# An AdaLN, RWKV and mixture-of-experts block: routing weights spread over 64 partitions by DMA in place of selection products

## The reference, cut to what matters

```
logits = x @ gate_w.T                                  # (n, 8)
topk_vals, topk_idx = jax.lax.top_k(logits, 2)
w = jax.nn.softmax(topk_vals, axis=-1)
comb = jnp.zeros((n, E), x.dtype).at[jnp.arange(n)[:, None], topk_idx].add(w)
g = jnp.einsum('nh,ehm->enm', x, Wg)                   # 8 experts of M = 64
u = jnp.einsum('nh,ehm->enm', x, Wu)
eo = jnp.einsum('enm,emh->enh', jax.nn.silu(g) * u, Wd)
y = jnp.einsum('ne,enh->nh', comb, eo)
y = y + jax.nn.silu(x @ sWg) * (x @ sWu) @ sWd         # the shared expert, 128 wide
```

## Time and profile before

| what | value |
|---|---|
| runs shown | 423.52, 424.86, 425.09 us; median 424.86 us |
| profiled execution, its own time | 426.54 us |
| its span in the profile | 424.7 us |
| mean granted TensorE clock | 0.954 of full speed |
| TensorE busy | 377.9 us, 89% of the span |
| VectorE busy | 334.4 us, 79% |
| ScalarE busy | 294.6 us, 69% |
| GpSimd busy | 53.0 us, 12% |
| DMA moved | 13.27 MB, mean 31 GB/s |

### The profile page before, as it was taken

The page is one execution under the profiler, slowest core; times in us unless marked ns, Lnnn a source line. Parts: engine busy times, 40 slices in busy tenths (PEclk is TensorE's granted clock), DMA queues, the critical chain, the costliest instruction groups (busy, mean ns, idle before and its releaser), DMA issues.

```text
span 424.7 us, 4271 instructions
## 1 busy us (share of the span) xinstructions
PE 377.9 (89%) x1347; PEld 223.3 (53%) x1347; DVE 334.4 (79%) x661; ACT 294.6 (69%) x466; POOL 53.0 (12%) x80
## 2 busy tenths in 40 slices
PE   0796196399999999999999999999999999979985
PEld 0745142375546564646465645565465546645742
DVE  1597979896989799869988898969897988661541
ACT  1576949974899479956996699848993787334332
POOL 2111344000220013000500050002200200010000
PEclk9996579689999999999999999999999999989999
DMA  7900001000100020001100110002000100100011
GB/s 269 264 1 2 1 0 49 0 2 0 50 0 2 0 99 2 2 0 55 45 0 2 51 49 0 2 14 85 2 1 0 49 2 0 49 2 0 0 51 49
DMA packets 15626, 13.27 MB, mean 31 GB/s; under 512 B 4690, under 2 KB 15092, under 8 KB 15604
## 3 DMA queue, kind: packets, MB, share of 16 engines
q1 hardware_dynamic: 14464, 11.94, 9.2%
q10 hardware_dynamic: 1140, 1.06, 0.8%
HBM read 8.80 MB, written 4.19 MB: 31 GB/s over the span
## 4 chain that ended last, share of the span: by engine, by line
PE 73%; ACT 14%; DVE 7%; issue 3%; DMA 1%; ACTq 1%; POOL 0%; DVEq 0%
PE mm L707 19%; PE mm L602 18%; PE yo L735 17%; PE yo L620 7%; PE yo L629 3%; ACT mixed L381 3%; PE cb L719 2%; PE tp L556 2%; ACT yT L448 2%; ACT L480 2%; ACT sgm L428 1%; DMA rows<-in_L_attn_bo_dram 1%; ACT arg L387 1%; PE yo L783 1%; ACT pool_g L434 1%
## 5 line engine op out<-in xcount | busy, mean ns | idle before, releaser
L602 PE MATMUL mm<-mixed,WT 128*128 128x512 f32 x192 | 89.0, 603 | 3.8 <-DVE mixed L845 3.8
L735 PE MATMUL yo<-act,w_dn 128*128 128x512 f32 x160 | 73.0, 605 | 3.8 <-DVE act L1022 3.8
L707 PE MATMUL mm<-h_h,w_up_h 128*128 128x512 f32 x160 | 61.0, 463 | 1.4 <-DVE h_l L945 1.4
L602 PEld LDWEIGHTS mm<-mixed,WT 128*128 128x128 f32 x192 | 34.7, 189 | 45.2 <-issue 40.0
L735 PEld LDWEIGHTS yo<-act,w_dn 128*128 128x128 f32 x160 | 30.3, 194 | 39.7 <-issue 35.0
L707 PE MATMUL mm<-h_l,w_up_h 128*128 128x512 f32 x160 | 51.2, 401 | 0.0
L707 PE MATMUL mm<-h_h,w_up_l 128*128 128x512 f32 x160 | 51.0, 400 | 0.0
L370 ACT ACTIVATE kv<-mm,cols 128x512 f32<-128x512 f32 x32 | 22.0, 688 | 39.6 <-PE mm L602 39.6
L290 POOL TENSOR_TENSOR n_ve<-n_mv,small 128x4 f32<-128x4 f32 x16 | 6.8, 424 | 304.8 <-DVE n_mv L834 304.8
L620 PE MATMUL yo<-pool_n,WT 128*128 128x512 f32 x64 | 31.9, 646 | 8.2 <-DVE pool_n L923 5.7
L845 DVE SCALAR_TENSOR_TENSOR mixed<-hT,cols,mixed 128x512 f32<-128x512 f32 x48 | 37.3, 821 | 0.5 <-ACT mixed L381 0.5
(11 more groups left out here) (143 smaller groups left out, 672.6 us busy)
## 6 DMA issues: line engine op xcount, KB each, us to landing
x_in<-in_L_attn_x_dram SPq DMA_DIRECT2D x8, 512.0 KB, 3.5
out_dram<-pool_x SPq DMA_DIRECT2D x5, 512.0 KB, 2.9
pool_x<-in_L_wmod_dram SPq DMA_DIRECT2D x2, 512.0 KB, 6.4
out_dram<-x_third SPq DMA_DIRECT2D x2, 512.0 KB, 2.9
pool_x<-in_L_wmod_dram SPq DMA_DIRECT2D x2, 256.0 KB, 4.4
pool_g<-in_L_ffn_Wg_dram SPq DMA_DIRECT2D x2, 256.0 KB, 7.6
pool_g<-in_L_ffn_Wu_dram SPq DMA_DIRECT2D x2, 256.0 KB, 5.6
w_dn<-in_L_ffn_Wd_dram SPq DMA_DIRECT2D x1, 512.0 KB, 4.2
```

The lines of the kernel that those rows point to most:

```text
L602: last = nc.tensor.matmul(mm[PROJECT_BANK[j]][:, :], WT[:, w, kc, oc * P:(oc + 1) * P], mixed[:, w, kc, :], start=(kc == 0), stop=(kc == K ...
L707: last = nc.tensor.matmul(mm[UP_BANK[i]][:, :], w[:, kc, gu, e * P:(e + 1) * P], rhs[:, kc, :], start=(n == 0), stop=(n == 3 * KH - 1))
L735: last = nc.tensor.matmul(yo[oc][:, :], w_dn[:, e, oc * P:(oc + 1) * P], act[:, e, :], start=(e == 0), stop=(e == NB - 1))
```

## The change

The two float32r halves, the matrix `sel` and the four products per chunk go. `comb` is kept as one float32 value (8 columns), `combT` has 8 partitions, and eight DMAs per chunk, issued by SyncE, copy each row of `combT` (one partition, 512 floats, 2 KB) to 64 partitions of a new SBUF tile `weights`. `weigh` reads `weights` and waits for the two DMAs of its block (`spread_in`). Two steps of `route` go, and `turn2` waits for `combT_done` where it waited for `act_done`, since `tp` and `cb` are no longer read by `weigh`. The new function `spread(n)` stands on SyncE ahead of `store(n - 1)` and `load(n + 3)`.

```diff
             def store(c):
                 sp.wait_ge(x2_done, 2 * (c.n + 1))
                 sp.dma_start(out_chunks[c.n], x1[c.n % 3][:, :, :]).then_inc(stored[c.n % 3], 16)
+
+            def spread(c):
+
+                sp.wait_ge(combT_done, c.n + 1)
+                for i in range(NP):
+                    wait(sp, act_done, NP * (c.n - 1) + i + 1)
+                    for e in range(2):
+                        sp.dma_start(weights[e * M:(e + 1) * M, i, :],
+                                     combT[2 * i + e:2 * i + e + 1, :].unsqueeze(1).to_broadcast([1, M, CH])
+                                     ).then_inc(spread_in[i], 16)
...
-            for n in range(NC - 1):
+            for n in range(NC):
+                spread(chunk(n))
+                if n:
+                    store(chunk(n - 1))
                 if chunk(n + 3):
                     load(chunk(n + 3))
-                store(chunk(n))
...
             def comb_out(c):
                 ac.wait_ge(comb_turned, c.n + 1)
-                nc.scalar.activation(combT[:, :], cb[0:2 * E, :], ACT.Identity).then_inc(combT_done, 1)
+                for i in range(NP):
+                    wait(ac, spread_in[i], 32 * c.n)
+                nc.scalar.activation(combT[:, :], cb[0:E, :], ACT.Identity).then_inc(combT_done, 1)
...
                 pe.wait_ge(norm2.xn_done, TT * (c.n + 1))
                 if c.n:
-                    pe.wait_ge(act_done, NP * c.n)
+                    pe.wait_ge(combT_done, c.n)
...
-            def spread_comb(c, e):
-
-                if e == 1:
-                    pe.wait_ge(combT_done, c.n + 1)
-                elif e < 4:
-                    pe.wait_ge(act_done, NP * c.n + e - 1)
-                nc.tensor.matmul(comb_bank[e][:, :], sel[:, e - 1, :], combT[:, :], start=True, stop=True
-                                 ).then_inc(comb_mm, 1)
...
-                    elif n == 16:
-                        ins = V.tensor_tensor(pr, w1m, w2m, ALU.add)
-                    elif n == 17:
-                        ins = V.tensor_copy(comb[:, :, 0:E], pr)
                     else:
-                        V.tensor_tensor(comb[:, :, E:2 * E], pr, comb[:, :, 0:E].bitcast(F32), ALU.subtract
-                                        ).then_inc(comb_done, 1)
+                        V.tensor_tensor(comb[:, :, :], w1m, w2m, ALU.add).then_inc(comb_done, 1)
                         return
...
             def weigh(c, e):
-                ve.wait_ge(comb_mm, NP * c.n + e)
+                ve.wait_ge(spread_in[e - 1], 32 * (c.n + 1))
                 ve.wait_ge(prod_done, NB * c.n + e + 1)
-                nc.vector.tensor_tensor(act[:, e, :], comb_bank[e][:, :], sg[:, e, :], ALU.mult).then_inc(act_done, 1)
+                nc.vector.tensor_tensor(act[:, e, :], weights[:, e - 1, :], sg[:, e, :], ALU.mult).then_inc(act_done, 1)
```

More of the change, by code:

```diff
@@ L59, in adaln_rwkv_moe @@
         ident = sb("ident", [P, P])
-        sel = sb("sel", [2 * E, NP, P], F32R)
         prio = sb("prio", [P, TT, E])
@@ L100, in adaln_rwkv_moe @@
         r1 = sb("r1", [P, 7, TT])
-        comb = sb("comb", [P, TT, 2 * E], F32R)
-        combT = sb("combT", [2 * E, CH], F32R)
+        comb = sb("comb", [P, TT, E])
+        combT = sb("combT", [E, CH])
+        weights = sb("weights", [P, NP, CH])
         lgT = sb("lgT", [2 * E, CH])
@@ L117, in adaln_rwkv_moe @@
         sg = pool_g[:, :].rearrange("p (e n) -> p e n", e=NB)
-        sel_f = tmp[0:2 * E, 0, :].rearrange("p (i n) -> p i n", i=NP)
         rec = arg[:, 0, :, :]
@@ L127, in adaln_rwkv_moe @@
         cb = ctx.enter_context(nc.psum_tensor("cb", [P, CH], F32))
-        comb_bank = {1: cb, 2: cb, 3: cb, 4: tp}
         UP_BANK = (0, 1, 2, 3, 0, 3, 0, 1, 2, 0)
@@ L157, in adaln_rwkv_moe @@
             sem(n) for n in ("rows_in", "mod_in", "mod2_in", "sq_in", "up_in", "dn_in", "gw_in"))
-        consts_done, ident_done, sel_done = sem("consts_done"), sem("ident_done"), sem("sel_done")
+        consts_done, ident_done = sem("consts_done"), sem("ident_done")
         cols_turned, cols_done, cond_done, fall_done, consts2_done = (
@@ L202, in adaln_rwkv_moe @@
         combT_done = sem("combT_done")
-        comb_mm = sem("comb_mm")
+        spread_in = [sem(f"spread_in{i}") for i in range(NP)]
         up_mm = sem("up_mm")
@@ L216, in adaln_rwkv_moe @@
         bias_cols = (col["bk"], col["bv"])
-        ROUTE_STEPS = 18
+        ROUTE_STEPS = 16
         N_CONSTS2 = 4
@@ L269, in _ @@
             nc.gpsimd.memset(ident[:, :], 0.0).then_inc(consts_done, 1)
-            nc.gpsimd.memset(sel_f[:, :, :], 0.0).then_inc(consts_done, 1)
             nc.gpsimd.memset(small[:, 0, :], EPS).then_inc(consts_done, 1)
@@ L273, in _ @@
             nc.gpsimd.memset(small[:, 2, :], 0.0).then_inc(consts_done, 1)
-            pool.wait_ge(consts_done, 5)
+            pool.wait_ge(consts_done, 4)
             nc.gpsimd.affine_select(out=ident[:, :], in_=ident[:, :], compare_op=ALU.not_equal, fill=1.0,
                                     base=0, pattern=[[-1, P]], channel_multiplier=1).then_inc(ident_done, 1)
[L278 to L284, removed]
             def rstd(norm, c):
@@ L667, in turn_comb @@
                 for t in range(TT):
-                    last = nc.tensor.transpose(cb[0:2 * E, t * P:(t + 1) * P], comb[:, t, :].bitcast(F32),
-                                               ident[:, :])
+                    last = nc.tensor.transpose(cb[0:E, t * P:(t + 1) * P], comb[:, t, :], ident[:, :])
                 last.then_inc(comb_turned, 1)
@@ L712, in spread_comb @@
             @of_chunk
-            def spread_comb(c, e):
-                if e == 1:
-                    pe.wait_ge(combT_done, c.n + 1)
-                elif e < 4:
-                    pe.wait_ge(act_done, NP * c.n + e - 1)
-                nc.tensor.matmul(comb_bank[e][:, :], sel[:, e - 1, :], combT[:, :], start=True, stop=True
-                                 ).then_inc(comb_mm, 1)
-            @of_chunk
             def down(c, oc):
@@ L763, in step @@
                 up(prev, 7)
-                spread_comb(prev, 1)
                 up(prev, 8)
                 turn_attn(cur)
-                spread_comb(prev, 2)
                 project(nxt, (2,))
                 up(prev, 9)
-                spread_comb(prev, 3)
                 project(nxt, (3,))
-                spread_comb(prev, 4)
                 project(nxt, (4, 5))
@@ L1068, in _ @@
             nc.vector.memset(hT[0][:, :, 0:1], 0.0)
-            ve.wait_ge(sel_done, 2)
-            nc.vector.tensor_copy(sel[:, :, :], sel_f[:, :, :])
             ve.wait_ge(cols_turned, 1)
```

## The result

The change makes the kernel slower: 686.63 us (four runs, 683.27 to 687.83) against 424.84 us, a ratio of 1.616 with a 95% interval of 1.6094 to 1.6225. 701 us were forecast, in a range of 620 to 820.

What follows compares the result with a forecast made beforehand. TensorE was taken as the bound (89% busy, 44.7 us steps). Waiting for eight transfers per chunk at 5.0 us each adds 276.5 us to 426.54, giving 703.0, less 1.7 for the median: 701 us, range 620 to 820.

Steps and rivals of the forecast that it cites:

- s: Price of one 131,072-byte weights transfer from one SBUF partition, taken as 5.0 us; the forecast covers 3.8 to 6.8 us.
- The estimate of 685 us: Alternative whole time from the skill's 27.6 GB/s for partitions 0 to 3: 4.75 us per transfer, about 685 us.
- W: End of `weigh` 4 on VectorE: T + 11.95 before, forecast T + 47.5 with store and load, T + 42.0 without load.
- behind the last two Ws: After chunk 7's last `weigh`, the cold clock of the last products was to add 1.7 us.
- T: End of ScalarE's write of `combT` in a step, 195.38 us in the pattern step; offsets count from it.
- the cold clock: TensorE's products after some 10 us idle run at the lower of two clocks, costing 1.9 us at `down`.
- Issued at once: All eight transfers of a chunk issued together, about 0.4 us per issue; block i's weights land at T + 1.4 + 10 i.
- Rival 1: Sixteen engines read one partition side by side, 1.15 us gained per step in six full ones: 419 us, chance 0.09.
- VectorE has slack for `weigh` 1: Rival 1's step on VectorE: `weigh` 1 waits 0.6 us, W slips to 207.9, `down` starts at 208.0 instead of 209.16.
- break-even: With s under about 1.0 us `down` isn't late; above it the kernel is slower.
- Rival 4: Stores and loads overtake the spreading transfers: 5.5 us less in five steps, 673 us; a variant inside the forecast's 0.80.

## Why the prediction was right

**The choice that carried it** was s, the price of one transfer, taken as 5.0 us between 4.7 and 5.3, on the reading that one source partition gives what one engine carries. It measured 4.85 us. The mechanism was near, but named too narrowly: not one partition but a group of four neighbours shares that rate, since four of them gave 25.5 GB/s together, and rows in different groups were read side by side. Nor is it one engine's rate, since a quarter of the engines drew as much from the group as sixteen did. That the two rates lie close together (24.8 GB/s for an engine by the earlier trace rows, 27.0 measured) made the number right, and that part was luck. The estimate of 685 us, from the 27.6 GB/s that the Trainium skill gives in "SBUF — State Buffer", section "Door 1: The DMA port swizzle (why `[64,N]` ≈ `[32,N]`)", was closer than my sum.

**Where the 14 us between 701 and 687 lie.** The sum was made for the profiled executions: 276.5 us more were forecast, 260.3 measured (426.54 to 686.80 us). The 16.2 between them, read from the timelines of the two kernels:

| stretch | forecast | measured |
|---|---|---|
| W's delay, eight chunks | 274.8 us | 255.2 us |
| W to the next L623, six steps | 0 | 4.7 us |
| behind the last two Ws | 1.7 us | 3.0 us |
| up to the first T (105.42 us before, 102.78 after) | 0 | -2.6 us |

W came at T + 42.5 in chunk 0 (46.0 forecast), at T + 44.7 to T + 44.8 in chunks 1 to 4 (47.5), and at T + 39.9 in chunks 5 to 7 (42.0). The last `weigh` of chunk 5, whose T is 493.61 us:

```profile
532.84 0.69 DVE L1005 TENSOR_TENSOR act<-weights,pool_g 128x512 f32<-128x512 f32 x1 [7.71 <-DMA weights<-combT]
```

It begins at T + 39.2, where the forecast had 41.4. Of these 2.2 us, 1.2 are eight times the 0.15 us of s. The other 1.0 was gained at T + 20, where the rows change from partition 3 to 4 and transfers overlapped. The store and the load, which I had put one behind the other with 3.7 us after the last weights, took 3.2. In chunk 5, which has no load, I had also taken the old W at T + 11.95; it was at T + 10.89.

A part of the 4.7 us behind W is the cold clock: it cost the first half of `down` 6.83 - 4.46 = 2.4 us in this step, not 1.9. My 1.9 had set a timeline's 6.22 against the 4.29 of a chain, which leaves out the overlap with the product ahead.

**Issued at once** was wrong, without a price. SyncE is held at each issue once a few transfers are queued, for 26.8 us per chunk. Since the store and the load stood behind the transfers either way, nothing came later by it.

**Rival 1 was put too low.** It gave 419 us if the transfers ran side by side, and a gain up to s of about 1.0 us. With the source in 64 partitions, issued every 0.6 us and landed in 2.4, the kernel took 430 us, and its step is 44.67 us (L624 at 180.80 and 225.47), what it was before (44.74). The step of the sum that failed is that VectorE has slack for `weigh` 1: in this kernel

```profile
195.52 0.69 DVE L1006 TENSOR_TENSOR act<-weights,pool_g 128x512 f32<-128x512 f32 x1 [1.49 <-DMA weights<-rows]
```

it waits 1.49 us there, and in this step W comes at T + 13.2, 1.3 us later than before. From W to the next L624 are then 19.6 us in place of 20.95, so that the two cancel. Without any transfer a step is 1.7 us shorter, not 2.4 nor the 2.2 that I expected of that run, since VectorE is the bound by then. The sum also had only 1 us lost at the end, where nothing is gained: up to T of chunk 5 the profiled execution of this kernel is 1.3 us ahead of the one before (328.77 and 330.09 us), and from there to the end of the span it takes 99.4 us in place of 94.6. So the change, with its transfers issued as here, did not win even with a source that is read at 200 GB/s. This weakens no part of the forecast, whose case was the slow one, but the break-even that it named was not there.

**The other steps.** The waits of `weigh` and `stats1`, their order and number, the DMA share near full at 27 GB/s, the lower clock at each `down`, and single VectorE durations as before (0.69 against 0.68 us for `weigh`) all came as described. Rival 4, loads that overtake, did not come about in the one queue; its price was right, though: 27.5 us less by the forecast, 26.6 less with the loads on a queue of their own.

## What to carry to other kernels

Before a DMA takes over a spread over partitions, ask which partitions its source lies in: rows on four neighbouring partitions were read at 25 to 27 GB/s, by sixteen engines and by a quarter of them. The same rows four partitions apart went about twice as fast, and a source of 64 partitions over seven times; from DRAM a transfer landed after 3.0 us in place of 17.6. Ask as well what stands behind it in its queue, here the loads of the next chunk. And price the gain against the engine that comes second: the products took 2.4 us of TensorE per step, and removing them altogether was worth 1.7. What a transpose does anyway can be the better way: spreading the column in the transpose itself took 8.5 us off.

## What the hardware showed that was not expected

- The DMA busy share reads 0.92 while 27 GB/s move; 1.02 stood beside 396 GB/s before. A full share doesn't mean a full rate.
- Transfers from one group of four partitions follow each other at 27 GB/s; where the source passes to the next group, 84 to 96 GB/s move for one microsecond.
- SyncE's issue of a DMA takes 0.46 us with an empty queue and up to 4.87 us with several transfers of 128 KB in it; for four-partition transfers it is 0.64 us at least.
- One queue can keep several source groups at work: with eight rows in eight groups it moves 57 to 78 GB/s, although each transfer reads a single partition.
- A matrix product with 16 rows of weights in front of a 128-row one leaves 0.19 us behind it; transposes of 128 x 128 leave none.
